# Row halves for the scores and 64x32 tiles for the values in a decoder layer on one Trainium2 core

## The reference

```python
qh, kh, vh = split(q @ Wq + bq), split(k @ Wk + bk), split(v @ Wv + bv)   # 16 heads x 8
logits = jnp.einsum('bhsd,bhtd->bhst', qh, kh) / jnp.sqrt(8)              # s = 1024, t = 6404
attn = jax.nn.softmax(logits, axis=-1)
out = jnp.einsum('bhst,bhtd->bhsd', attn, vh).reshape(...) @ Wo + bo
```

## Time and profile before

| | |
|---|---|
| runs | 880.16, 888.84, 880.13 us; median 880.16 |
| the profiled execution | 880.61 us |
| its span, first to last instruction | 878.6 us |
| mean granted TensorE clock | 0.971 of full speed |
| PE, PEld, DVE, ACT, POOL busy | 828.0, 318.9, 135.2, 789.5, 36.3 us |
| exponentials L641 | 536, from 103.4 us to the start of the last at 831.8 us |

### The profile page before, as it was taken

One profiled execution on the slowest core, in us unless ns is written; L12 is line 12 of the kernel. 1 busy time (PEld: TensorE's weight loads), 2 busy tenths in 40 slices (PEclk: granted clock), 3 DMA queues, 4 the chain that ended last, 5 costly groups with the idle time before them and its releaser, 6 DMA issues.

```text
span 878.6 us, 26636 instructions
## 1 busy us (share of the span) xinstructions
PE 828.0 (94%) x11146; PEld 318.9 (36%) x11148; DVE 135.2 (15%) x389; ACT 789.5 (90%) x651; POOL 36.3 (4%) x45
## 2 busy tenths in 40 slices
PE   6988799999999999999999999999999999999951
PEld 3436333333333333333333333333333333333331
DVE  3638500001000100010001000100000000000076
ACT  2446799999999999999999999999999999999942
POOL 2602400000000000000000000000000000000000
PEclk9998899999999999999999999999999999999965
DMA  3223511111111111111111111111111111111000
GB/s 107 65 63 119 180 53 41 40 59 41 41 42 59 44 42 41 56 43 42 43 55 44 44 41 52 48 43 40 49 51 42 42 42 59 41 42 40 12 1 24
DMA packets 24695, 44.63 MB, mean 51 GB/s; under 512 B 2566, under 2 KB 13992, under 8 KB 24640
## 3 DMA queue, kind: packets, MB, share of 16 engines
q1 hardware_dynamic: 23772, 43.31, 14.9%
q10 hardware_dynamic: 868, 0.48, 0.2%
HBM read 37.36 MB, written 6.42 MB: 50 GB/s over the span
## 4 chain that ended last, share of the span: by engine, by line
PE 81%; ACT 6%; issue 5%; DVE 4%; DMA 1%; POOL 1%; SPq 0%; ACTq 0%; POOLq 0%; DVEq 0%
PE ps L1172 38%; PE ps L1183 36%; ACT probs L641 5%; PE ps L1091 2%; PE ps L1077 2%; PE ps L1225 1%; DVE stats L692 1%; DMA q_parts_dram<-q_parts 1%; PE ps L1040 1%; DMA q_op<-shift_dram 1%; PE ps L1305 0%; POOL k_parts L494 0%; PE ps L1019 0%; PE ps L1043 0%; DVE probs L971 0%
## 5 line engine op out<-in xcount | busy, mean ns | idle before, releaser
L641 ACT ACTIVATE probs<-ps 128x1536 f32<-128x1536 f32 x536 | 724.6, 1555 | 8.4 <-PE ps L1172 6.9
L1172 PE MATMUL ps<-q_op,k_op 96*32 96x512 bf16 x6400 | 444.5, 382 | 3.8 <-DMA q_op<-shift_dram 3.5
L1183 PE MATMUL ps<-probs,v_op 128*9 128x512 f32 (+1 forms) x4288 | 446.3, 492 | 0.3 <-ACT probs L641 0.3
L1172 PEld LDWEIGHTS ps<-q_op,k_op 96*32 96x32 bf16 x6400 | 149.3, 95 | 346.8 <-ACT probs L641 242.0
L1183 PEld LDWEIGHTS ps<-probs,v_op 128*9 128x9 f32 x4288 | 109.9, 91 | 121.7 <-issue 1.6
L857 DVE COPY v_op<-v_all 128x108 f32 (+1 forms) x136 | 36.1, 265 | 601.9 <-PE ps L1183 600.4
L598 ACT ACTIVATE probs<-ps,neg_n 128x1024 f32<-128x1024 f32 x8 | 8.9, 1113 | 16.8 <-PE ps L1091 16.8
L1040 PE MATMUL ps<-ctx_t,wk_turned 128*128 128x384 f32 x34 | 16.5, 569 | 6.2 <-ACT ctx_t L550 3.2
L494 POOL TENSOR_TENSOR k_parts<-probs,k_parts 128x384 bf16<-128x384 f32 x17 | 17.4, 1026 | 61.9 <-ACT k_parts L571 61.9
L1043 PEld LDWEIGHTS ps<-wv_sb,ctx_t 128*128 128x128 f32 x102 | 15.5, 208 | 5.2 <-issue 1.2
L558 ACT ACTIVATE kf<-ps,bias_cols 128x384 f32<-128x384 f32 x17 | 9.8, 577 | 8.3 <-PE ps L1040 8.2
(11 more groups left out here) (168 smaller groups left out, 209.1 us busy)
## 6 DMA issues: line engine op xcount, KB each, us to landing
k_op<-k_parts_dram SPq DMA_DIRECT2D x408, 72.0 KB
k_parts_dram<-k_parts SPq DMA_DIRECT2D x17, 288.0 KB, 3.0
ctx_nat<-in_ctx_dram SPq DMA_DIRECT2D x16, 192.0 KB, 2.6
q_op<-q_parts_dram SPq DMA_DIRECT2D x24, 96.0 KB
q_parts_dram<-q_parts SPq DMA_DIRECT2D x2, 384.0 KB, 4.5
x_nat<-in_x_dram SPq DMA_DIRECT2D x1, 512.0 KB, 3.8
out_dram<-res SPq DMA_DIRECT2D x1, 320.0 KB, 2.7
out_dram<-res ACTq DMA_DIRECT2D x1, 192.0 KB, 2.8
```

The source lines that it names most:

```text
L641: act.activation(probs[:, s], ps[:, 3 * (s % 2):3 * (s % 2) + 3, :], ACT.Exp, scale=SCALE).then_inc(probs_ready, 1)
L1172: last = pe.matmul(ps[a:a + P // G, bank, :], k_op[0:KR, kslot, k, P * j + a:P * j + a + P // G], q_op[0:KR, q, k, :], start=True, stop=Tr ...
L1183: last = pe.matmul(ps[32 * k:32 * k + DH + 1, ACC[ph % 2], a:b], v_op[:, slot, j, (DH + 1) * k:(DH + 1) * (k + 1)], probs[:, (first_block ...
```

## The change

The score operand takes 59 rows (56 of parts and 3 of shift) instead of 96, and stands twice: heads 0 and 2 of a group at partitions 0 to 58, heads 1 and 3 at partitions 64 to 122. A unit's scores are then one matmul of a 64-row half by 128 columns. A tile's values are eight matmuls of 64 rows by 32 columns: each head's 128 keys in two halves, the upper accumulating in bank 6, the lower in bank 7. Both banks serve every phase, so DVE adds them, and PE's first values of a phase wait until that is done (`acc_free`); they now come a whole chunk after their scores. DVE turns the sum by its own 32x32 transposes, divides and turns it back, and SP writes the rows to `o_t` by DMA, four per phase. Staging moves from DVE to POOL. `load_k` issues 6 DMAs instead of 3, `load_q` 8 instead of 4. In the tail the first half's projection stands ahead of the last values.

```diff
-KR = 96
+R2 = 2
+G2 = G // R2
+KR = 59
+W2 = P // R2
+V_AHEAD = 2 * VPC
...
         def load_k(sp, slot, chunk, group, signal, counter=None, count=None):
...
-            for a in range(3):
-                sp.dma_start(k_op[32 * a:32 * a + 24, slot, :, :].rearrange("p k t -> p (k t)"),
+            for r in range(R2):
+                for a, b, parts in ((0, 24, 3), (24, 40, 2), (40, 56, 2)):
+                    sp.dma_start(k_op[W2 * r + a:W2 * r + b, slot, :, :].rearrange("p i t -> p (i t)"),
+                                 bass.AP(src.tensor, starts[r],
+                                         [[P * CK, parts], [G2 * CK, DH], [1, G2 * CK]])
+                                 ).then_inc(signal, 16)
...
+            def stage(slot, m, tile, head):
+                pool.wait_ge(v_ready, NC + 1)
+                pool.wait_ge(values_done, m * VPC + VPC)
+                pool.tensor_copy(
+                    v_op[:, slot].rearrange("p j (h d) -> p j h d", h=G),
+                    v_all[:, bass.ds(tile, CT), head:head + G, :]).then_inc(v_staged, 1)
...
+            def add_acc(ph):
+                dve.wait_ge(values_done, V_AHEAD + VPC * NC * (ph + 1))
+                acc_chain.step(dve.tensor_copy(acc_sb[:], ps[:, ACC[0], :]))
+                acc_chain.step(dve.tensor_tensor(acc_sb[:], acc_sb[:], ps[:, ACC[1], :], ALU.add))
+            for ph in range(PHASES - 1):
+                add_acc(ph)
+                acc_chain.step(dve.transpose(acc_t[:].rearrange("p n d -> p (n d)"), acc_sb[:]))
+                dve.sem_inc(acc_free, 1)
...
+            def score(kslot, q, bank, j, k, a, b):
+                i, r = divmod(k, R2)
+                return pe.matmul(ps[a:b, bank, :],
+                                 k_op[W2 * r:W2 * r + KR, kslot, i, P * j + a:P * j + b],
+                                 q_op[W2 * r:W2 * r + KR, q, i, :], start=True, stop=True,
+                                 skip_group_check=True)
...
+            def values(slot, first_block, j, last_chunk, count=1, first=False, a=0, b=HQ):
+                packed = last_chunk and j == CT - 1
                 for k in range(G):
+                    block, u = divmod(j * G + (0 if packed else k), BU)
+                    for h in range(R2):
+                        if packed and h != k // G2:
+                            continue
+                        last = pe.matmul(ps[32 * k:32 * k + DH + 1, ACC[h], a:b],
+                                         v_op[W2 * h:W2 * h + W2, slot, j, (DH + 1) * k:(DH + 1) * (k + 1)],
+                                         probs[W2 * h:W2 * h + W2, (first_block + block) % NP, u, a:b],
+                                         start=first, stop=True, skip_group_check=True)
...
+                    if c == 0:
+                        if s < CT:
+                            values(slot, f - LAST_BPC, s, True, count=2 if s == 1 else 1)
+                    elif c == NC - 1:
+                        values(slot, f - BPC, s, False, count=2 if s == 1 else 1)
+                    elif s == 0:
+                        if c == 1 and ph:
+                            pe.wait_ge(acc_free, ph)
+                        values(slot, f - BPC, 0, False, first=c == 1)
+                    elif s == 3:
+                        values(slot, f - BPC, 2, False)
                     else:
-                        values(1 - slot, ph, f - BPC, 1, False, a=s * (HQ // 4), b=(s + 2) * (HQ // 4))
-                    if c == 1 and s == 2:
-                        turn_acc(1 - q, ph + 1)
+                        values(slot, f - BPC, 1, False, a=(s - 1) * (HQ // 2), b=s * (HQ // 2))
...
+            pe.wait_ge(probs_ready, BLOCKS + 1)
+            project_out(0)
+            pe.wait_ge(v_staged, PHASES * NC)
             for j in range(CT):
                 pe.wait_ge(probs_ready, BLOCKS + min(j + 1, 2))
```

More of the change, by code:

```diff
@@ L256, in load_q, with load_k @@
-        def load_q(sp, slot, half, group_rows, group, signal, counter=None, count=None):
-            src = q_parts_dram[half, 0, group_rows, :].rearrange("(d k) t -> d (k t)", k=G)
-            src = bass.AP(src.tensor, sp.snap(src.offset), [[P * HQ, 3]] + [list(v) for v in src.ap])
+        def load_k(sp, slot, chunk, group, signal, counter=None, count=None):
+            src = k_parts_dram[chunk, 0, group, :]
+            rows = P // (NG * R2)
+            starts = [sp.snap(src.offset + r * (rows * CK)) for r in range(R2)]
@@ new lines, in _, with load @@
+            for ph in range(PHASES):
+                half, g = divmod(ph, NG)
+                f0 = ph * BPP
+                def load(slot, before, chunk, group):
+                    load_k(sp, slot, chunk, slice(32 * group, 32 * group + 32), k_loaded[slot],
+                           scores_done, before + AHEAD)
+                with sp.Fori(0, NC // KS - 1) as r:
+                    for k in range(KS):
+                        load((ph + k) % KS, f0 + r * (KS * BPC) + (k + 1) * BPC, r * KS + (k + KS), g)
+                load(ph % KS, f0 + (NC - KS) * BPC, NC - 1, g)
+                if ph < PHASES - 1:
+                    after = (g + 1) % NG
+                    load_q(sp, 1 - ph % 2, (ph + 1) // NG, slice(32 * after, 32 * after + 32), after,
+                           q_loaded[1 - ph % 2])
+                    for k in range(KS):
+                        done = BPP if k == KS - 1 else (NC - KS + k + 1) * BPC
+                        load((ph + 1 + k) % KS, f0 + done, k, after)
+                if ph:
+                    half, g = divmod(ph - 1, NG)
+                    sp.wait_ge(att_ready, ph)
+                    for k in range(G):
+                        sp.dma_start(o_t[32 * g + DH * k:32 * g + DH * k + DH, HQ * half:HQ * half + HQ],
+                                     att_rows[32 * k:32 * k + DH, :]).then_inc(o_written, 16)
@@ L1219, in chunk @@
[L1219 to L1229 removed]
+                        wait(k_loaded[(m + 1) % KS], at(K_LOAD * ((m + 1) // KS + 1), K_LOAD // KS))
@@ L1279, in _ @@
             last.then_inc(pe_tail, 1)
+            pe.wait_ge(att_ready, PHASES)
+            for st in range(4):
+                last = pe.matmul(ps[32 * (NG - 1):P, 1, P * st:P * st + P],
+                                 last_att[:, st].rearrange("p k d -> p (k d)"), ident[:],
+                                 start=True, stop=True)
+            last.then_inc(pe_tail, 1)
+            pe.wait_ge(act_tail, 1)
+            pe.wait_ge(o_written, 16 * G * (PHASES - 1))
             project_out(1)
```

270 lines of the change are left out of this document (110 added, 160 removed).

## The result

The changed kernel takes 891.63 us (median of four runs, 890.71 to 892.64), the kernel before 880.14 on the same chip. The ratio is 1.0124, with an interval of 1.0078 to 1.017: **slower by 1.2%**, 3.6 us above the forecast of 888. (One of the four runs of before took 888.84 us, over 8 us more than the others; the median of the four hardly feels it, and no trace says why.) The profiled execution took 890.71 us, its span is 889.0 us against 878.6, and the mean granted clock is 0.970 against 0.971.

A forecast was written before the change was run, and what follows sets the result against it. ACT was taken as the bound inside a phase. Phase ends +6.0, loop start -1.0 and tail +3.1 sum to +8.1 us on the profiled 880.6, so 888.7, or 888 us as a median; range 875 to 910.

The forecast's parts named there:

- ACT stays the bound inside a phase: Inside a phase: exponentials stay 1.343 us apart; PE's chunk takes 5.35 us against ACT's 5.37, 0.02 to spare.
- Scores in two waves, values unchanged: PE, each block: scores take two waves, 0.43 us, saving 0.21; values stay 0.86 for a whole tile.
- Changes of shape: PE, each block: changing tile shape and back adds 0.11 + 0.10 + 0.05 = 0.26 us, bounds 0.05 and 0.33.
- The end of a phase: Seven phase ends: whole tiles 1.16 us plus accumulators' wait 0.65, 1.8 against 1.0 before; +6.0 us in all.
- Start of the loop: First chunks: low-clock time partly regained, chunk 4's keys 0 to 1.5 us late; sum -1.0, between -2.5 and +2.
- SP in the loop: SP's queue: six DMAs issued in about 4.2 us per chunk of 5.37, covered, cost 0.
- Tail: After the loop: projection about 1.1 us, DVE pass 0.7, matmuls for transposes 0.8, last exponential 0.55 late; +3.1 us.
- rival 1: Shape changes cost a block over 0.265 us, PE becomes the bound everywhere: 905 us at 0.30, 920 at 0.33; chance 0.21.
- the second: Rival on PE: no pause between 64x128 and 64x32 tiles, 878 us; chance 0.17.
- the third: Rival on PE's scores: the two row halves don't run at once, scores 0.65 us, about 985 us; chance 0.06.
- the fourth: Rival on ACT's pace: its 1.343 us is partly PE's doing, 871 or 881 us; chance 0.08.
- The fifth: Rival on TensorE's clock: the granted clock falls to half inside the loop, over 1300 us; chance 0.02.

The follow-up runs named there:

- experiment 8: The changed kernel with ACT's exponential over two of a block's three banks, so PE sets the pace: 881.44 us, a chunk on PE 5.28 us.
- Experiment 7: The changed kernel with the scores' row half chosen by the block instead of by the head: 1072.44 us.
- experiment 5: The kernel before with each unit's scores as one matmul 128 columns wide instead of four of 32: 982.0 us.
- experiment 2: The changed kernel with each unit's scores as four 64x32 matmuls, the values' tile shape: 879.96 us, ratio to before 1.0012.
- experiment 12: The four edits together, but with SP's four last stores of keys between the loads of chunks 2 and 3: 876.44 us, ratio to before 0.9973.
- experiment 1: The changed kernel with SP's four last stores of keys moved ahead of the loads of chunks 2 and 3: 889.92 us, ratio to before 1.013.
- the third run of experiments 8 to 10: The changed kernel with scores as 64x32 matmuls and ACT's exponential over two of three banks: 880.18 us.
- experiment 4: The changed kernel with the tail's first-half projection behind the last values, and DVE's first residual addition behind the last division: 890.09 us, ratio to before 1.0124.
- experiments 6 and 7: The changed kernel with all scores read from row half 0 (1667.92 us), and with the row half chosen by the block (1072.44 us).
- the four edits: To the changed kernel: 64x32 scores, acc_free signalled before DVE's transposition, key stores earlier, tail projection behind the last values; together 875.7 us, ratio to before 0.9963.
- two of the single runs: The kernel before with 128-column scores (982.0 us), and the changed kernel with 64x32 scores and exponentials over two of three banks (880.18 us).

## Why the prediction was nearly right, and which step was not

- **ACT stays the bound inside a phase**: right. Its pace is 1.343 as before, and PE's own chunk is 5.28 us, not 5.35, with 0.09 to spare, not 0.02 (experiment 8).
- **Scores in two waves, values unchanged**: right. Experiment 7 prices the wave saved at 0.215 us.
- **Changes of shape, 0.26 a block**: 0.24 in the changed kernel's trace, 0.22 in experiment 5. The step on which the sign rests; experiment 2, which takes them away, gives 10.8 us of span back. The pause of 0.09 to 0.10 was right, 0.10 to 0.14; the 0.02 of weight load and 0.05 of start were not told apart.
- **The end of a phase**, 1.8 against 1.0 and +0.85: measured 91.75 - 67 x 1.3433 = 1.75 against 0.97, and +0.78 a phase, so +5.5 for seven against the forecast's +6.0. Two errors nearly cancel in it: the accumulators' wait was put at 0.65 and is 0.82 (2.16 less 1.34), so the rest was put at 1.16 and is 0.93. DVE's transposition, for which no row stood, takes 0.71; 0.65 had been taken.
- **Start of the loop**, forecast -1.0: **this is the term that failed.** The first phase is 3.02 us longer, of which about 0.6 is its own end; and the first exponential is 0.2 earlier: +2.2. It put chunk 4's keys "near 123, just when PE comes to it: 0 to 1.5 lost". They came at 125.8. The stores ended where it said (114.6), but it left out that the writes themselves take over 4 us, and that the first load behind them is issued only then. And it left out the clock: here 3.4 us at 0.54 followed the stand of 2.5 us (in experiment 12 none followed one of 2.51). With the stores moved (experiment 1) the first phase is about 92.5 without its end, against 92.94: the gain of the first chunk is there, some 0.45 of it with the late keys still in.
- **SP in the loop**, six DMAs "in about 4.2 us per chunk": 5.0 to 5.1 with the steps between. It cost nothing in the changed kernel's later phases, as forecast, but it left 0.3 us a chunk to catch up instead of 1.2, and became the bound of the third run of experiments 8 to 10.
- **Tail**, +3.1: measured 2.2 behind the last exponential and 0.5 at the end of the last phase, 2.7. The projection cost 1.1 as predicted (1.06 by the copy's distance from the last exponential, 1.13 by experiment 4), the addition 0.71; the matmuls in place of transposes 0.4, half of what was taken.

The sum: 5.5 + 2.2 + 2.7 = 10.4, as measured between the two spans; 8.1 was forecast. That is 2.3 of the 3.6 us by which the median was missed; the rest lies between the profiled executions and the medians.

One price of the prediction was reckoned wrong: with 0.30 for the changes, a chunk on PE is 5.51 by its own terms, not 5.45, so rival 1 would have cost about 16 + 7 us there, 911, and the range's upper end of 910 stood for a change of 0.30, not 0.31. The result doesn't hang on it. Of the rivals, the first (PE becomes the bound) was 0.09 us a chunk away and did not come; the second falls to experiments 2 and 5, the third to experiment 7; the fourth did not come in the changed kernel, whose chunks take 5.373 us, and is not settled beyond it (experiment 2). The fifth, half clock in the loop, had been given 0.02 with the argument that PE is as busy as before; experiments 6 and 7 show low clock with PE wholly busy, so that argument was wrong though the outcome was not.

## What to carry to other kernels

A cheaper matmul is only as cheap as its neighbours let it be: where two shapes alternate in every block, count about 0.11 us for each change first, and try the new row split in the old column width. Look at what else the edit moves: one by one, the four edits give back 10.8 us for the shape and 5.2, 1.1 and 2.9 for the other three (by spans and phases; 15.7 together), so nearly half lay outside the matmuls: a signal sent one DVE pass too late, a projection ahead of a wait that could have covered it, and a queue of six DMAs where three stood. For a queue, follow each transfer to its landing, not its issue.

## What the runs showed of the hardware

- The granted clock can stay at 0.50 with PE busy 300.00 of 300.00 us: it did so for the whole loop when all scores used one row half, and for 190 us when the halves took turns by the block. The changed kernel, with two halves at once, had 1.00 from 112 us on, but for 3.4 us near 127. Not settled why.
- TensorE ran part of the setup at half pace in two of the single runs (four 32x512 f32 matmuls 3.62 us, elsewhere 1.90) while its granted clock reads 1.00 for the stretch. It puts the loop 8 to 10 us later.
- The same stand had two outcomes: after 2.5 us for a DMA the changed kernel's clock was 0.54 for 3.4 us; after 2.51 us in experiment 12 it was 1.00.
- A chunk of four exponentials has two even paces, 5.32 us (1.330 each) and 5.373 (1.343 on the mean), in the kernels that ACT bounds. A phase runs some chunks at 5.32 after a disturbance and then goes to 5.373; with all scores 64x32 (experiment 2) it stays at 5.32 for most of the phase, and with the four edits together for a few blocks only. That is 3 to 7 us over the loop, and stays open.
- A tile group of one shape can start while another of the same shape still streams in the other row half: values 0.24 us behind scores whose stream is 0.43 (experiment 2).
- A chunk's keys in six DMAs of 16 or 24 rows cost SP 0.70 us each at the start (18 in 12.53) and about 0.83 in the loop, with the steps between. With three DMAs of 24 rows it was 0.92 in the loop with the steps between. In the loop the issue of 24 rows takes 0.75, of 16 rows 0.63 to 0.67: fewer rows are hardly cheaper, so twice as many DMAs cost 1.8 times as much.
